# Scores summed over key differences in half-depth matmuls, and two maxima products moved into the batch ahead

## The reference, cut to what matters

```
q_big = _apply_rope(einsum('bshk,hkq->bshq', q_hk, w_kc_q), sin_q, cos_q)
kv_r  = _apply_rope(kv_c, sin_k, cos_k)                # 1444 keys of 64 features
q_r   = einsum('bshq,hqr->bhsr', q_big, W_qr)
k_r   = einsum('bld,hdr->bhlr', kv_r, W_kr)
scores = einsum('bhsr,bhlr->bhsl', q_r, k_r)
attn  = softmax(scores)
ctx_c = einsum('bhsl,bld->bhsd', attn, kv_r)           # then two projections
```

## Time and profile before

| | us |
|---|---|
| median of 3 runs | 3590.11 |
| lowest, highest | 3571.32, 3590.87 |
| the profiled execution | 3590.73 |
| its span, first to last instruction | 3588.9 |
| PE busy | 3053.0 (85%) |
| DVE busy | 2329.4 (65%) |
| POOL busy | 1556.9 (43%) |
| ACT busy | 1339.3 (37%) |

### The profile page before, as it was taken

The page is one execution under the profiler, slowest core; times in us unless marked ns, Lnnn a source line. Parts: engine busy times, 40 slices in busy tenths (PEclk is TensorE's granted clock), DMA queues, the critical chain, the costliest instruction groups (busy, mean ns, idle before and its releaser), DMA issues. The chain is left out here.

```text
span 3588.9 us, 55868 instructions
## 1 busy us (share of the span) xinstructions
PE 3053.0 (85%) x16648; PEld 2035.5 (57%) x16656; DVE 2329.4 (65%) x3226; ACT 1339.3 (37%) x2810; POOL 1556.9 (43%) x1035
## 2 busy tenths in 40 slices
PE   6999879998699989989989998998998999897244
PEld 4777679997455545555555564555555556454123
DVE  5777754454766666666666666666666666664887
ACT  1322322222144344424424434443443443443356
POOL 0000022221554545544645554554554555553566
PEclk9988889999899999989999999999999999998566
DMA  3000010002100000000000000000000000000100
GB/s 103 0 0 0 0 49 9 5 9 51 28 19 17 17 13 20 16 10 20 21 8 20 16 17 13 21 15 15 15 21 9 21 15 17 8 14 26 67 12 24
DMA packets 129556, 70.00 MB, mean 20 GB/s; under 512 B 83566, under 2 KB 123854, under 8 KB 129224
## 3 DMA queue, kind: packets, MB, share of 16 engines
q1 hardware_dynamic: 129288, 66.79, 7.4%
HBM read 56.30 MB, written 10.04 MB: 18 GB/s over the span
## 5 line engine op out<-in xcount | busy, mean ns | idle before, releaser
L1080 POOL TENSOR_TENSOR c_psum<-c_p 120x800 f32<-120x800 f32 (+1 forms) x384 | 749.1, 1956 | 807.1 <-ACT c_p L1298 513.1
L1139 DVE TENSOR_REDUCE c_mneg<-c_m_ps 128x1 fp32r<-128x1452 f32 (+1 forms) x448 | 745.3, 1664 | 407.5 <-PE c_m_ps L1340 406.8
L1298 ACT ACTIVATE c_p<-c_s_ps 120x400 f32<-120x400 f32 (+1 forms) x1536 | 655.0, 509 | 774.9 <-PE c_s_ps L1424 772.8
L1437 PE MATMUL c_o_ps<-c_p,c_val 120*64 120x400 f32 (+1 forms) x3072 | 598.8, 511 | 0.0
L1423 PE MATMUL c_s_ps<-c_q,c_k 128*120 128x400 f32 (+1 forms) x1536 | 576.3, 375 | 10.1 <-ACT c_q L1246 8.8
L1424 PE MATMUL c_s_ps<-c_q,c_k 128*120 128x400 f32 (+1 forms) x1536 | 536.4, 349 | 0.0
L1340 PE MATMUL c_m_ps<-c_k,c_q 64*128 64x484 f32 (+1 forms) x1344 | 328.7, 445 | 131.8 <-DVE c_mneg L1139 104.7
L1073 POOL TENSOR_TENSOR c_rot<-c_psum,c_rs 96x400 f32<-96x400 f32 x256 | 259.9, 1038 | 308.5 <-DVE c_rs L1181 304.9
L1423 PEld LDWEIGHTS c_s_ps<-c_q,c_k 128*120 128x120 f32 (+1 forms) x1536 | 283.3, 184 | 178.5 <-issue 161.7
L1437 PEld LDWEIGHTS c_o_ps<-c_p,c_val 120*64 120x64 f32 (+1 forms) x3072 | 187.0, 136 | 275.0 <-issue 143.1
L1340 PEld LDWEIGHTS c_m_ps<-c_k,c_q 64*128 64x128 f32 (+1 forms) x1344 | 130.7, 175 | 347.0 <-DVE c_mneg L1139 233.4
(11 more groups left out here) (220 smaller groups left out, 4161.4 us busy)
## 6 DMA issues: line engine op xcount, KB each, us to landing
c_rdb<-l_denominators SPq DMA_DIRECT2D x128, 100.0 KB, 2.7
c_kv<-in_ctx SPq DMA_DIRECT2D x32, 360.0 KB
c_q<-c_mneg SPq DMA_DIRECT2D x384, 0.5 KB, 1.9
c_den<-c_oden SPq DMA_DIRECT2D x256, 0.8 KB
x_rows<-in_x SPq DMA_DIRECT2D x4, 800.0 KB
x_spill<-x_rows SPq DMA_DIRECT2D x8, 400.0 KB
...
```

The costliest lines, as they stand in the source:

```text
L1080: g.tensor_tensor(psum[0:k, u % 2, :], p[0:k, 2 * u % 4, :], p[0:k, (2 * u + 1) % 4, :], ALU.add).then_inc(psum_ready, 1)
L1139: v.tensor_reduce(mneg[0:n, c, t:t + 1], m_ps[0:n, :, 0:4 * KP], AX.XY, ALU.max, negate=True).then_inc(mneg_ready, 1)
L1298: a.activation(p[0:k, w % 4, i * HALFQ:(i + 1) * HALFQ], s_ps[0:k, (2 * w + i) % 4, 0:HALFQ], ACT.Exp).then_inc(exp_ready, 1)
L1437: mm = pe.matmul(o_ps[i * DL:(i + 1) * DL, 0:HALFQ], val[0:k, j % 2, r, :], p[0:k, w % 4, i * HALFQ:(i + 1) * HALFQ], start=(r == 0), stop ...
```

## The change

- **Scores.** The keys are held as differences: for a tile r of 2 and over, `kd` holds keys of tile r less keys of tile r - 2, made by five subtractions on POOL (`difference`). Tiles r - 2 and r use the same PSUM bank, and the matmuls of tile r now add to what tile r - 2 left there. So the negated maximum is added in tiles 0 and 1 of a chunk alone, by one more matmul for each half (`first` by `mrow`).
- **Half depth.** Each half of the chunk has its own 64 rows of the array: rows 0:64 make columns 0 to 399, rows 64:128 columns 400 to 799, each with rounded differences by rounded queries, their remainders by rounded queries, and rounded differences by the queries' remainders. That is six matmuls of depth 64 for a tile (eight in tiles 0 and 1) where there were four of depth 128. PE waits once for a tile, for both exponentials two tiles back, where it waited for each half alone.
- **Maxima.** They take keys of their own (`kmax`: rows 0:64 copied by DVE in `round_keys`, rows 64:128 by ACT), and no longer wait for the keys of the scores. The seventh product has 128 queries too (96 of them again). The first two products of a second chunk move from slots 0 to 8 of their batch to slots 21 and 22 of the batch ahead (`EARLY`); j = 0 keeps its seven.
- **Copies.** ACT makes nine copies of a third of the keys each (`round_steps`) beside tiles 14 to 21 of the batch ahead (`TILE_STEPS`), or in steps 10 to 15 of the head, where it made three; DVE's three remainders (`split_keys`) move from slot 9 to behind `invert` in the second chunk (pair 9), or to step 12 of the head.
- **DMAs.** The row of maxima goes to `mrow`; the fourth product's row is cut in two, so a chunk has eight such DMAs where it had seven.

```diff
@@ beside
-        FIRST, LATER, NEXT = (1, 2, 3, 4, 6, 7, 8), (0, 1, 3, 4, 6, 7, 8), (12, 13, 15, 16, 18, 19, 20)
+        FIRST, LATER, NEXT, EARLY = (1, 2, 3, 4, 6, 7, 8), (0, 3, 4, 6, 8), (12, 13, 15, 16, 18, 19, 20), (21, 22)
...
-                return ("max", j, 1, later.index(slot))
+                return ("max", j, 1, NQT - len(later) + later.index(slot))
+            if slot in EARLY and j + 1 < G:
+                return ("max", j + 1, 1, EARLY.index(slot))
+        HEAD_STEPS = {10: (0, 1), 11: (2,), 12: (3,), 13: (4, 5), 14: (6, 7), 15: (8,)}
+        TILE_STEPS = {14: (0,), 15: (1,), 16: (2,), 17: (3, 4), 18: (5,), 19: (6,), 20: (7,), 21: (8,)}
@@ POOL
+                def difference(b, r):
...
+                    new, old = slice(r * KP, (r + 2) * KP), slice((r - 2) * KP, r * KP)
+                    g.tensor_tensor(kd[:, new], kd[:, new], kd[:, old], ALU.subtract).then_inc(kd_ready, 1)
...
+                        if j + 1 < G and at in (5, 6):
+                            for r in ((10, 8, 6), (4, 2))[at - 5]:
+                                difference(b + 1, r)
@@ DVE
+                def round_keys(b):
+                    v.wait_ge(kf_ready, PRIMED + b * 3 + 1)
+                    v.tensor_copy(klow[:, 0:4 * KP], m_ps[0:DL, 0, 0:4 * KP]).then_inc(kmax_low, 1)
+                    v.wait_ge(kf_ready, PRIMED + b * 3 + 3)
+                    v.tensor_copy(klow[:, 8 * KP:12 * KP], m_ps[0:DL, 2, 0:4 * KP]).then_inc(kmax_low, 1)
...
-                        v.wait_ge(k1_hi, PRIMED + b * 3 + k + 1)
-                        v.tensor_tensor(k1[j % 2][DL:128, cols], m_ps[0:DL, k, 0:4 * KP], k1[j % 2][0:DL, cols].bitcast(F32),
+                        v.wait_ge(k1_hi, PRIMED + b * 6 + k + 1)
+                        v.sem_inc(m.carrier, 1)
+                        v.tensor_tensor(k2[j % 2][0:DL, cols], kd[:, cols], k1[j % 2][0:DL, cols].bitcast(F32),
...
                         if (j, c) != (0, 0) and q == 2:
                             invert(ch - 1)
+                        if j + 1 < G and (c, q) == (1, 2):
+                            split_keys(it * G + j + 1, j + 1)
@@ ACT
+                def round_steps(b, j, n):
+                    cols = slice(n % 3 * 4 * KP, (n % 3 + 1) * 4 * KP)
+                    if n < 6:
+                        a.wait_ge(kd_ready, PRIMED + (b + 1) * 5)
+                        a.sem_inc(m.carrier, 1)
+                        a.activation(k1[j % 2][n // 3 * DL:(n // 3 + 1) * DL, cols], kd[:, cols], ACT.Copy).then_inc(k1_hi, 1)
+                    else:
+                        a.wait_ge(k1_ready, PRIMED + b * 3 + n - 5)
+                        a.sem_inc(m.carrier, 1)
+                        a.activation(k2[j % 2][DL:128, cols], k2[j % 2][0:DL, cols].bitcast(F32), ACT.Copy).then_inc(k2_ready, 1)
@@ PE, scores
+                        if w >= 2:
+                            pe.wait_ge(exp_ready, PRIMED + 2 * it * NU + 2 * w - 2)
...
+                        if r < 2:
+                            for i in range(2):
+                                pe.matmul(bank[i][0:KP], first[side[i], :], mrow[side[i], c, :], start=True, stop=False, skip_group_check=True)
                         for i in range(2):
...
-                            pe.matmul(o, k1[j % 2][:, r * KP:r * KP + k], q1[:, j, cols], start=True, stop=False)
-                            mm = pe.matmul(o, k2[j % 2][:, r * KP:r * KP + k], q2[:, j, cols], start=False, stop=True)
-                            mm.then_inc(s_ready, 1)
+                            pe.matmul(bank[i][0:k], k1[j % 2][side[i], keys], q1[side[i], j, q[i]], start=False, stop=False, skip_group_check=True)
+                        for i in range(2):
+                            pe.matmul(bank[i][0:k], k2[j % 2][side[i], keys], q1[side[i], j, q[i]], start=False, stop=False, skip_group_check=True)
+                        for i in range(2):
+                            pe.matmul(bank[i][0:k], k1[j % 2][side[i], keys], q2[side[i], j, c, :], start=False, stop=True, skip_group_check=True).then_inc(s_ready, 1)
```

More of the change, by code:

```diff
@@ L838, in phase_l1_attention @@
     NQT = len(QT)
+    starts = [128 * t for t in range(NQT - 1)] + [CQS - 128]
     NU = G * CH * NT
@@ L966, in load_row @@
                         sp.sem_inc(m.carrier, 1)
-                        sp.dma_start(q2[0:1, j, c * CQS + t * 128:c * CQS + t * 128 + QT[t]].bitcast(F32), mneg[0:QT[t], c, t:t + 1].bitcast(F32)).then_inc(row_loaded[c], 16)
+                        q0, q9 = 128 * t, 128 * t + QT[t]
+                        for half in range(2):
+                            lo, hi = max(q0, half * HALFQ), min(q9, (half + 1) * HALFQ)
+                            if lo < hi:
+                                sp.dma_start(mrow[half * DL:half * DL + 1, c, lo - half * HALFQ:hi - half * HALFQ].bitcast(F32),
+                                             mneg[lo - starts[t]:hi - starts[t], c, t:t + 1].bitcast(F32)).then_inc(row_loaded[c], 16)
                 def store_rows(b, j, more):
@@ L1068, in head @@
                         n = gi * H + i
+                        if i in (5, 6, 7, 8, 9):
+                            difference(gi * G, NT - 2 - 2 * (i - 5))
                         if i >= 4:
@@ L1095, in _ @@
                 g.memset(ones[:], 1.0).then_inc(consts, 1)
-                for i in range(2):
-                    g.memset(k2[i][0:DL, :].bitcast(F32), 1.0).then_inc(consts, 1)
+                g.memset(first[:].bitcast(F32), 0.0).then_inc(consts, 1)
+                g.wait_ge(consts, PRIMED + 2)
+                for half in range(2):
+                    g.memset(first[half * DL:half * DL + 1].bitcast(F32), 1.0).then_inc(consts, 1)
+                g.wait_ge(consts, PRIMED + 2 + 2)
                 deviation(0)
-                g.memset(q2[0:DL].bitcast(F32), 0.0).then_inc(consts, 1)
+                g.memset(mrow[:].bitcast(F32), 0.0).then_inc(consts, 1)
                 g.wait_ge(t_loaded, 16 * 4)
@@ L1298, in group @@
                                 a.activation(p[0:k, w % 4, i * HALFQ:(i + 1) * HALFQ], s_ps[0:k, (2 * w + i) % 4, 0:HALFQ], ACT.Exp).then_inc(exp_ready, 1)
-                            if w % CT in (10, 11, 12) and j + 1 < G:
-                                place_keys(it * G + j + 1, j + 1, w % CT - 10)
+                            for n in TILE_STEPS.get(w % CT, ()) if j + 1 < G else ():
+                                round_steps(it * G + j + 1, j + 1, n)
                         if (j, c) != (0, 0) and q == 0:
@@ L1335, in maxima @@
                 def maxima(b, j, c, t):
-                    ch, n = b * CH + c, QT[t]
-                    pe.wait_ge(mneg_ready, PRIMED + ch * NQT + t)
-                    low, high, full = (slice(0, DL), k1), (slice(DL, 128), k2), (slice(0, 128), k1)
-                    for k, (rows, keys) in enumerate((low, high, low) if n == 128 else (full, full, full)):
-                        mm = pe.matmul(m_ps[0:n, k, 0:4 * KP], q1[rows, j, c * CQS + t * 128:c * CQS + t * 128 + n],
-                                       keys[j % 2][rows, k * 4 * KP:(k + 1) * 4 * KP], start=True, stop=True)
+                    pe.wait_ge(mneg_ready, PRIMED + (b * CH + c) * NQT + t)
+                    low, high = slice(0, DL), slice(DL, 128)
+                    q = slice(c * CQS + starts[t], c * CQS + starts[t] + 128)
+                    pe.matmul(m_ps[:, 0, 0:4 * KP], q1[low, j, q], klow[:, 0:4 * KP], start=True, stop=True)
+                    pe.matmul(m_ps[:, 1, 0:4 * KP], q1[high, j, q], khigh[:, 4 * KP:8 * KP], start=True, stop=True)
+                    mm = pe.matmul(m_ps[:, 2, 0:4 * KP], q1[low, j, q], klow[:, 8 * KP:12 * KP], start=True, stop=True)
                     mm.then_inc(maxs_ready, 1)
```

93 lines of the change are left out of this document (53 added, 40 removed).

## The result

| | before | changed kernel |
|---|---|---|
| median us (lowest to highest) | 3582.93 (3571.32 to 3590.87) | 3745.81 (3735.18 to 3765.02) |
| span of the profiled execution | 3588.9 | 3733.4 |
| a group, first scores of its first pair to those of its last, median of 8 | 216.5 | 236.2 |

The ratio is 1.046 (95% interval 1.041 to 1.052): 163 us slower, where 60 faster was forecast. The groups hold it: in the two profiled executions their eight lengths add up to 1730 and 1894 us, 164 more, and the heads between them to 6 more. (The spans differ by less, 144, since the first group began at 989 us before and at 964 after; its start lies between 964 and 989 us in all the profiled executions, those of the kernel before with small edits too.)

The account below looks back on a forecast made before the run. PE looked like the bound, but its waits for reductions keep products at least 2.47 us apart. Eight groups at -8.6 give -69, the heads +8: 3590.7 - 61 = 3530 us, range 3480 to 3605.

Parts of the forecast that it names:

- What bounds the kernel: Attention phase: PE looks like the bound but waits 100.5 us for reductions; two maxima products are never closer than 2.47 us.
- the clock: Sign to watch: PE's clock stays at 0.99 in the groups; if longer idle stretches lowered it, every term is too small.
- The half-depth scores: PE's scores: two half-depth matmuls take one slot, 0.183 us; a pair of tiles costs 1.10 us, 0.36 less.
- rival C: PE's scores: two half-depth matmuls do not share the array fully, 0.60 us more per tile pair, 134 us, 3666 us; 8%.
- j = 3: Batch without next keys, late or early products: pairs 1 to 6 fall from 28.7 to 24.1 us, whole batch 6.4 less.
- the multiplication at 0.57 us: Pair 5, DVE: the multiplication after the inversion, ahead of the last reduction, was counted at 0.57 us.
- 12.6 + 4.97 + 0.57 + 1.65 = 19.8: Pair 5, DVE: inversion at 12.6, 4.97 to the multiplication, 0.57 for it, 1.65 for the last reduction, ending at 19.8 us.
- the remainders at 1.75: Late half, DVE: three remainders between SBUF tiles behind the inversion add 1.75 us.
- a half refund of 0.35: Late half, DVE: an addition takes 1.69 us beside POOL where 0.98 is usual; half of that taken back, 0.35.
- Rival D: DVE stands still for its remainders' inputs from ACT and POOL, reductions queued behind; at 4 us late, 3626 us; 9%.
- hidden as long as the remainders do not wait for them: ACT's seven more copies per batch at 0.60 us and POOL's five subtractions, at most 1 us each, fit in idle time.
- The forecast for a group, 8.6 less: Four batches together: 1.0 more for j = 0, 3.2 less for j = 1 and 2, 6.4 less for the last.

Follow-up runs that it names:

- the move that ended it: Changed kernel with POOL's five key differences all made ahead of its addition in pair 6: 3696.1 us, 1.033.
- Filling two waits: Changed kernel with 16 matmuls of zero weights, adding nothing, ahead of PE's waits in slots 9 and 19: 3726.8 us, 1.042.
- the spread and held kernel: Changed kernel with POOL's differences earlier, DVE's remainders and multiplications moved and spread, and POOL's additions for pairs 5 and 10 held by waits: 3497.8 us, 0.976.
- the held additions: Changed kernel, order unchanged, with two waits more on POOL, ahead of its additions for pairs 4 and 10: 3641.1 us, 1.018.

## Why the prediction was wrong

**What bounds the kernel**: right. Pairs 1 to 4 of j = 1 were forecast at 14.7 us and measured 14.7 in the table's terms (with the matmuls of the negated maximum counted in 15.2; they are 14.7 in j = 2 and 3, where the clock stayed at 1.00). The half-depth scores cost what was said; rival C is false. j = 3 was 5.3 less (forecast 6.4): its multiplication, too, was long beside POOL, 2.19 us in the second group, and pair 6 took 7.8 where 6.1 was forecast.

**Failed, the multiplication at 0.57 us.** The step "12.6 + 4.97 + 0.57 + 1.65 = 19.8" came out as 13.2 + 4.85 + 2.25 + 1.66, with the joins 22.2 (1345.53 to 1367.70); the 13.2 holds another case of the same, DVE's addition ahead of the inversion, 1.46 us beside POOL where it takes 0.98. The row for 0.57 in the earlier trace rows is one from pair 11, where POOL was idle until 0.17 us after the multiplication had begun. POOL's addition, second there, was long instead (2.16 for 1.90); timeline of POOL, kernel before:

```profile
1394.99 2.16 POOL L1080 TENSOR_TENSOR c_psum<-c_p 120x800 f32<-120x800 f32 x1 [2.62 <-ACT c_p L1298]
```

In pair 5 of the kernel before POOL was first; DVE, and POOL beside it:

```profile
1362.03 1.65 DVE L1147 TENSOR_TENSOR c_ct<-c_onum,c_rdb 128x400 f32<-128x400 f32 x1
```

```profile
1361.35 4.06 POOL L1080 TENSOR_TENSOR c_psum<-c_p 120x800 f32<-120x800 f32 x2
```

All 64 multiplications of the kernel before, shortest, median and longest in ns:

```profile
L1147 DVE TENSOR_TENSOR c_ct<-c_onum,c_rdb x64: 557/1176/2189, 1039.3 to 3302.6; 128x400 f32<-128x400 f32 x64
```

The 40 that began while POOL was at work took 0.89 to 2.19 us, the other 24 took 0.56 to 0.58, also the 22 of them beside which POOL began later.

**Failed, the remainders at 1.75.** They took 3.81. The price was taken from the earlier trace rows, where one input comes from PSUM and POOL's work beside it was ending; with both inputs in SBUF and POOL beside them they are another operation. The prediction had the clue, DVE's addition of 1.69 "beside POOL where 0.98 is usual", and booked it as a half refund of 0.35 instead of asking what POOL does to whatever stands there next. The Trainium skill has this rule (SBUF — State Buffer, "Who interferes with whom"): a DVE instruction with two inputs in SBUF and a GpSimd instruction that reads SBUF exclude each other, and the one issued first goes first. The trace agrees in the main: beside an addition of POOL that had begun, the multiplication ended 0.43 us and the second remainder, by its own row below, 0.52 us after it, nearly their whole own length (0.57 and 0.65).

```profile
1396.78 2.32 DVE L1173 TENSOR_TENSOR c_k<-c_kd,c_k 64x484 fp32r<-64x484 f32 x1
```

The prediction did not weigh this rule.

**Missed, a wait in front of somebody else's work.** Rival D had DVE standing for its inputs; DVE never did. It was ACT that stood for POOL's differences, in pair 8, and PE that waited for the copy queued behind on ACT. It cost 1.0 to 2.0 us a batch, 39 us by pair 8's lengths; the move that ended it measured 50. The sentence that ACT's and POOL's work is "hidden as long as the remainders do not wait for them" named one waiter and not the other.

**Missed, the clock.** The prediction named it as what would spoil every term and priced it at nothing. Behind the waits of 4.03 and 4.96 us in j = 1, and behind one of 1.92 us in pair 8 of j = 2, stretches at its lower level (1.2 GHz) followed. Pair 6 of j = 1 took 8.2 us instead of 6.1, and 6.7 with the wait ahead of it filled. Filling two waits gave back 19 us in sum.

For j = 1 these make up, within 0.4 us, the miss of 10.9 us. Pairs 5 and 6: 5.8 (2.4 until the transposes, 1.3 in them, 2.1 in pair 6). Pair 8: 2.0. Pair 10: 2.4. Pairs 11 and 12: 1.4, there too an addition long beside POOL (1.99) and reductions behind a late start. Pair 7 gave 0.6 back, pair 9 took 0.3. The forecast for a group, 8.6 less, is near what the spread and held kernel reached (207.4 where 216.5 was, 9.1 less). That the two agree is partly luck, since that kernel has another order than the one forecast; what it shows is that the work to be saved was there. Two sums of the prediction are off by a rounding: pairs 1 to 6 of j = 3 add up to 24.0, not 24.1, and rival C to 3664, not 3666. How much of the 105 us of the held additions is shorter operations and how much the clock that falls less (0.93 in the groups for 0.92) was not separated.
